# Maxima ahead of scores: the order of two matmul pairs, and of the PSUM banks they take, in a two-layer transformer block

## The chip, the cores and the metric

The kernel runs on one core of a Trainium2 chip. The metric is the device time of one execution in microseconds (us). TensorE (PE) multiplies, VectorE (DVE) and ScalarE (ACT) read PSUM, GpSimd (POOL) works in SBUF and starts indirect DMAs, SyncE (SP) starts the other DMAs.

## The reference

Four sequences of 512 tokens of width 128 go through two layers. Each is `x = x + attention(layernorm(x)) + ffn(layernorm(x))`:

```
scores = einsum('bhqe,bhke->bhqk', q, k) * scale        # 16 heads of width 8
attn   = softmax(scores, axis=-1)                       # layer 1: with a block mask of 64x64 blocks
out    = einsum('bhqk,bhke->bhqe', attn, v) -> projection
layer 0 ffn: silu(x @ wg.T) * (x @ wu.T) @ wd.T         # 384 hidden, weights int / 127
layer 1 ffn: 8 experts, top 2 per token, at most CAP tokens per expert, 256 hidden each
```

Everything stays in f32 accuracy: q and k are held as sums of three bf16 parts.

## The kernel before, in words

One sequence in one layer is a **unit** u (0 to 3 are layer 0, 4 to 7 layer 1). A unit has 16 **slots**: four groups of heads (s) by four blocks of 128 keys (k). A slot has two **halves** (jj = 0, 1), and each half makes

- a **score** pair (`score_mms`, L733): two matmuls, keys on the partitions, 512 queries, from 59 rows of KO and QO. Three of the rows of QO carry minus the row maximum, so that ACT's exponential (`exponential`, L946, 128x1024 in one instruction) gives the softmax numerators in `PT`;
- a **maxima** pair (`max_mms`, L718): two matmuls, queries on the partitions, 512 keys, whose row maxima DVE takes (`read_max`, L1098, a reduce of 128x1024). These maxima belong to work 24 pairs (12 slots) ahead: from slot 4 of unit u on they are those of unit u + 1. In unit 7 only slots 0 to 3 have maxima.

Between the two halves PE multiplies the numerators of the slot before by the values (`value_mms`, L749, 8 matmuls); it waits for both exponentials of that slot. After the second half stands the slot's side work: transposes, q and k of a later unit (L681), output products, values of the next unit (L687 or L692), and in slots 9 to 11 of layer 0 the gate and up products (L771, L772; DVE's L1119 and L1134 use them). From slot 4 of unit 6 on each slot also holds two jobs of the experts (L778, L788, L789, L796; ACT's L969, L962, L978).

PSUM has eight banks. Bank 6 holds the values product, bank 7 the side work. The other six are three **pairs of banks**, handed out in turn: `taken` lists all jobs (scores, maxima, gates, expert jobs) in PE's order, the i-th takes pair i % 3, and `take_pair` makes PE wait until the job three places before it in the list has been read: a score by ACT's exponential (`exp_done`), a maxima pair by DVE's reduce (`max_read`), a gate job by DVE's last product (`h_ready`).

DVE and ACT have their own fixed orders, which the change leaves alone. In each slot DVE reads the first maxima, then does the side work that the slot has (softmax normalization in slots 2 and 11, residual in 7, layernorm statistics in 8, values in 9, router logits in 13), reads the second maxima, then does the gate products. ACT does the first exponential, side copies, and the second exponential. SP's queue starts the DMAs in one order: operand rows, rows of the maxima (L431), mask rows (L425), and in unit 0 the clearing of the expert buffers (L338, L341).

Of the kernel before, what the change touches and what calls it, by code (L numbers as in the profile page):

```python
# [17 lines left out]
def build(nc, x, wq, wk, wv, bq, bk, bv, wo, bo, wg_T, wu_T, wd_T, src_blocks, tgt_blocks, router_T, eg_T, eu_T,  # L18
# [33 lines left out]
    with ExitStack() as ctx:  # L52
# [191 lines left out]
        SLOTS_U = 16  # L244
# [6 lines left out]
        def layer(u):  # L251
            return u // B
# [12 lines left out]
        def rows_of(t, half, j, rows, blocks):  # L265

            return t[64 * half:64 * half + rows, j, blocks[0] * P:blocks[1] * P]

        def reads_of(u):

            return 16 * sum(4 if layer(v) == 0 else 32 for v in range(u % 3, u + 1, 3))

        def pairs_at(u, slot):

            q = LEAD + PAIRS_U * u + 2 * slot
            return [v for v in (q, q + 1) if v < N_PAIRS]

        def gate_at(u, slot):

            return HB * u + slot - 9 if u < B and 9 <= slot < 9 + HB else None  # L280
# [12 lines left out]
        def expert_work_at(u, slot):  # L293

            a = 2 * (SLOTS_U * (u - (U - 2)) + slot - EXPERTS_FROM)
            return expert_work[a:a + 2] if a >= 0 else []
# [6 lines left out]
        taken = [("max", q) for q in range(LEAD)]  # L303
        for u in range(U):
            for slot in range(SLOTS_U):
                for jj in range(2):
                    taken.append(("score", 2 * (SLOTS_U * u + slot) + jj))
                    if len(pairs_at(u, slot)) > jj:
                        taken.append(("max", pairs_at(u, slot)[jj]))
                if gate_at(u, slot) is not None:  # L310
                    taken.append(("gate0", gate_at(u, slot)))
                taken += expert_work_at(u, slot)
# [5 lines left out]
        def take_pair(pe, kind, n):  # L318

            i = turn[kind, n]  # L320
            if i >= 3:
                before, m = taken[i - 3]
                left = {"score": exp_done, "max": max_read, "gate0": h_ready[0], "gate1": h_ready[1],
                        "places": places_ready, "expert": y_copied}[before]
                pe.wait_ge(left, m + 1)
            return i % 3
# [376 lines left out]
        def max_mms(pe, q):  # L703
            u, m = q // PAIRS_U, q % PAIRS_U
            s, qt, jj = m // 8, m % 8 // 2, m % 2
            if m == 0:
                if u == 0:
                    pe.wait_ge(first_rows, 16 * 4)
                else:
                    pe.wait_ge(qk_rows[u % 3], reads_of(u))  # L710
                if B <= u < B + 3:
                    pe.wait_ge(mask_rows, 32 * (u - B + 1))
            if q == PAIRS_U // 2:
                pe.wait_ge(qk_rows[0], reads_of(0))
            pair = take_pair(pe, "max", q)
            rows = PROD_ROWS if layer(u) == 0 else M_ROW
            for half in range(2):
                mm = pe.matmul(ps[:, 2 * pair + half, :], rows_of(QO[u % 3], half, 2 * s + jj, rows, (qt, qt + 1)),  # L718
                               rows_of(KO[u % 3], half, 2 * s + jj, rows, (0, NT)), start=True, stop=True)
            mm.then_inc(max_ps, 1)  # L720
# [8 lines left out]
        def score_mms(pe, u, slot, jj):  # L729
            s, k = slot // 4, slot % 4  # L730
            pair = take_pair(pe, "score", 2 * (SLOTS_U * u + slot) + jj)
            for half in range(2):
                mm = pe.matmul(ps[:, 2 * pair + half, :],  # L733
                               rows_of(KO[u % 3], half, 2 * s + jj, ROWS, (k, k + 1)),
                               rows_of(QO[u % 3], half, 2 * s + jj, ROWS, (0, NT)), start=True, stop=True)
            mm.then_inc(st_ps, 1)

        def value_mms(pe, t):
            u, slot = t // SLOTS_U, t % SLOTS_U
            s, k = slot // 4, slot % 4  # L740
            pe.wait_ge(exp_done, 2 * t + 2)
            if slot == 0:
                pe.wait_ge(v_read, u + 1)
                if u >= 1:
                    pe.wait_ge(o_copied, 2 * u)
            if slot == 8:
                pe.wait_ge(o_copied, 2 * u + 1)
            for g in range(4):
                last = pe.matmul(ps[32 * g:32 * g + 32, PV_BANK, :], Vp[u % 2][:, k, head(s, g), :],  # L749
                                 PT[:, (2 * t + g % 2) % 4, g // 2, :],  # L750
                                 start=(s % 2 == 0 and k == 0), stop=(s % 2 == 1 and k == NT - 1))
            last.then_inc(pv_done, 1)
# [13 lines left out]
        def gate_up_0(pe, g):  # L766
            u, i = g // HB, g % HB
            pe.wait_ge(ready, 1)
            pair = take_pair(pe, "gate0", g)
            cols = slice(i * P, (i + 1) * P)  # L770
            pe.matmul(ps[:, 2 * pair, :], wg[:, cols], xnT[u % 4][:], start=True, stop=True).then_inc(gate_ps[0], 1)  # L771
            pe.matmul(ps[:, 2 * pair + 1, :], wu[:, cols], xnT[u % 4][:], start=True, stop=True).then_inc(up_ps[0], 1)  # L772

        def places_mms(pe, e):
            pe.wait_ge(places_in[e % 2], 16 * (e // 2 + 1))
            pair = take_pair(pe, "places", e)
            for j in range(JE):
                last = pe.transpose(across(pair, j * P, (j + 1) * P), places[e % 2][:, j, :], ident[:])  # L778
            last.then_inc(places_ps, 1)

        def gate_up_1(pe, g):

            e, i, c = g // 4, g % 4 // 2, g % 2
            pe.wait_ge(loaded, N_LOAD)
            pe.wait_ge(places_ready, e + 1)
            pair = take_pair(pe, "gate1", g)
            cols, x_T = slice(i * P, (i + 1) * P), places_T[e % 2][:, c * HALF:(c + 1) * HALF]
            pe.matmul(ps[:, 2 * pair, 0:HALF], eg[:, e, cols], x_T, start=True, stop=True).then_inc(gate_ps[1], 1)  # L788
            pe.matmul(ps[:, 2 * pair + 1, 0:HALF], eu[:, e, cols], x_T, start=True, stop=True).then_inc(up_ps[1], 1)  # L789
# [10 lines left out]
        def out_mms(pe, u, tiles):  # L800
            L = layer(u)
            if tiles[0] == 0:
                pe.wait_ge(onT_ready, u + 1)
                if L == 0:
                    pe.wait_ge(h_ready[0], HB * (u + 1))
            for t in tiles:
                tok = slice(t * P, (t + 1) * P)
                last = pe.matmul(ps[:, SIDE, tok], o_T[:, tok], w_proj[L][:], start=True, stop=(L == 1))
                if L == 0:
                    for i in range(HB):  # L810
                        last = pe.matmul(ps[:, SIDE, tok], h0_T[:, i, tok], wd[:, i, :], start=False,  # L811
                                         stop=(i == HB - 1))
            if tiles[-1] == NT - 1:
                last.then_inc(y_ps, 1)
# [70 lines left out]
        def tensor_unit(pe, u):  # L885
            pe.wait_ge(m_rows[0], 16 * M_DMAS * (u + 1))
            for slot in range(SLOTS_U):
                if slot == 8:
                    pe.wait_ge(m_rows[1], 16 * M_DMAS * (u + 1))
                maxima = pairs_at(u, slot)  # L890
                score_mms(pe, u, slot, 0)
                if maxima:
                    max_mms(pe, maxima[0])
                if u > 0 or slot > 0:
                    value_mms(pe, SLOTS_U * u + slot - 1)
                if slot == 6 and u >= 1:
                    pe.wait_ge(mT_ready, 2 * u + 2)
                    out_mms(pe, u - 1, (0, 1))
                score_mms(pe, u, slot, 1)
                if maxima:  # L900
                    max_mms(pe, maxima[1])
                if gate_at(u, slot) is not None:
                    gate_up_0(pe, gate_at(u, slot))
                for kind, n in expert_work_at(u, slot):
                    if kind == "places":
                        places_mms(pe, n)
                    elif kind == "gate1":
                        gate_up_1(pe, n)
                    else:
                        expert_out(pe, n)  # L910
                side_mms(pe, u, slot)
# [507 lines left out]
        def _(pe):  # L1419
# [27 lines left out]
            for u in range(U):  # L1447
                tensor_unit(pe, u)
# [52 lines left out]
```

## Time and profile before

| | us |
|---|---|
| median of 3 runs | 556.64 |
| lowest and highest | 556.34, 560.81 |
| the profiled execution: its time | 560.18 |
| the profiled execution: its span | 558.2 |

In the span PE is busy 82%, DVE 72%, ACT 59%, POOL 47%. The first 69 us load, lay out q and k of the first units and find the first maxima; the 128 slots run from there to about 520 us; the end gathers the experts' results. Matmuls are pipelined: a PE row's length holds its latency, so the distance from one start to the next tells what it costs.

### The profile page before, as it was taken

All of it is one profiled execution on the core that took longest, in us unless ns stands there. A gap on an engine that the chain in (4) does not pass through costs nothing.

```text
span 558.2 us, 9308 instructions
## 1 busy us (share of the span) xinstructions
PE 456.9 (82%) x3394; PEld 170.5 (31%) x3394; DVE 401.1 (72%) x535; ACT 328.4 (59%) x422; POOL 260.8 (47%) x502
## 2 busy tenths in 40 slices
PE   3165298989798899889988988898799999999952
PEld 2011022223332243224322422232135444555511
DVE  3589479987588879886898698779877877723304
ACT  2100267677357766776676567767776676667560
POOL 6525039104843537377728775786210333063240
PEclk9755599999799999999999999999999999999995
DMA  1698964589970045153615363445650111010018
GB/s 52 177 203 135 123 225 143 86 87 105 243 140 4 1 122 56 18 65 130 69 12 68 129 69 32 57 143 70 77 99 26 49 47 50 1 44 26 20 43 216
DMA packets 156511, 48.28 MB, mean 86 GB/s; under 512 B 115170, under 2 KB 153586, under 8 KB 155634
## 3 DMA queue, kind: packets, MB, share of 16 engines
q1 hardware_dynamic: 154162, 42.93, 43.1%
q0 software_dynamic: 2304, 4.76, 2.6%
q8 instruction: 27, 0.44, 0.3%
q14 instruction: 18, 0.15, 0.1%
HBM read 22.81 MB, written 23.14 MB: 82 GB/s over the span
## 4 chain that ended last, share of the span: by engine, by line
PE 48%; DVE 12%; SPq 11%; issue 10%; ACT 9%; DMA 7%; POOL 2%; POOLq 0%; ACTq 0%; DVEq 0%
PE ps L749 12%; PE ps L733 8%; PE ps L718 6%; ACT PT L946 6%; DVE mx L1098 5%; PE ps L788 3%; PE ps L796 3%; SPq L338 2%; PE ps L771 2%; DMA QO<-mT 2%; PE ps L789 2%; PE ps L681 2%; SPq L420 2%; PE ps L811 1%; PE ps L772 1%
## 5 line engine op out<-in xcount | busy, mean ns | idle before, releaser
L1098 DVE TENSOR_REDUCE mx<-ps 128x2 f32<-128x1024 f32 x256 | 309.5, 1222 | 86.4 <-PE ps L718 78.0
L946 ACT ACTIVATE PT<-ps 128x1024 f32<-128x1024 f32 x256 | 258.3, 1025 | 135.6 <-PE ps L733 126.6
L749 PE MATMUL ps<-PT,Vp 128*32 128x512 f32 x1024 | 138.1, 611 | 5.4 <-ACT PT L946 4.4
L718 PE MATMUL ps<-KO,QO 48*128 48x512 bf16 (+1 forms) x512 | 104.3, 407 | 45.4 <-ACT PT L946 22.0
L733 PE MATMUL ps<-QO,KO 59*128 59x512 bf16 x512 | 100.5, 391 | 13.7 <-DMA QO<-mT 13.7
L507 POOL DMA_INDIRECT y_tokens<-y_sb,meta x40 | 38.5, 963 | 71.6 <-ACT y_sb L978 48.4
L733 PEld LDWEIGHTS ps<-QO,KO 59*128 59x128 bf16 x512 | 24.6, 93 | 151.9 <-issue 96.3
L532 POOL CAST mp<-mx 128x32 bf16<-128x32 f32 x16 | 3.4, 214 | 100.1 <-DVE mx L1098 95.9
L718 PEld LDWEIGHTS ps<-KO,QO 48*128 48x128 bf16 (+1 forms) x512 | 25.5, 96 | 77.5 <-ACT PT L946 38.3
L1119 DVE SCALAR_TENSOR_TENSOR th<-th,ps 128x320 f32<-128x320 f32 (+1 forms) x44 | 23.8, 541 | 35.2 <-ACT th L962 29.4
L496 POOL DMA_INDIRECT x_places<-xe,place_i x32 | 31.9, 995 | 21.9 <-ACT PT L946 15.8
L749 PEld LDWEIGHTS ps<-PT,Vp 128*32 128x32 f32 x1024 | 20.4, 108 | 46.3 <-issue 40.4
L962 ACT ACTIVATE th<-ps 128x320 f32<-128x320 f32 (+1 forms) x44 | 21.1, 486 | 12.0 <-PE ps L788 5.5
L788 PE MATMUL ps<-places_T,eg 128*128 128x320 f32 x64 | 24.4, 463 | 2.2 <-ACT y_sb L978 0.7
L1134 DVE SCALAR_TENSOR_TENSOR h_all<-th,ps 128x320 f32<-128x320 f32 (+1 forms) x44 | 23.8, 541 | 1.5
L479 POOL TENSOR_SCALAR xe<-xs,mv,rstd 128x128 f32<-128x128 f32 x28 | 22.2, 804 | 0.8 <-POOL rstd L470 0.2
L789 PE MATMUL ps<-places_T,eu 128*128 128x320 f32 x64 | 22.4, 432 | 0.0
L978 ACT ACTIVATE y_sb<-ps,meta 128x128 f32<-128x128 f32 x40 | 11.2, 371 | 18.7 <-PE ps L796 18.7
L796 PE MATMUL ps<-ed,h_all 128*128 128x128 f32 x160 | 19.4, 276 | 1.2 <-DVE h_all L1134 1.2
L796 PEld LDWEIGHTS ps<-ed,h_all 128*128 128x128 f32 x160 | 18.9, 192 | 3.0 <-DVE h_all L1134 1.7
L939 ACT COPY mT<-ps 24x512 bf16<-24x512 bf16 x16 | 9.0, 561 | 16.2 <-PE ps L725 16.2
L1104 DVE RECIPROCAL rden<-ps 128x32 f32<-128x32 f32 x16 | 5.6, 348 | 16.8 <-PE ps L757 16.8
(167 smaller groups left out, 477.8 us busy)
## 6 DMA issues: line engine op xcount, KB each, us to landing
z<-part SPq DMA_DIRECT2D x16, 384.0 KB
z<-part SPq DMA_DIRECT2D x16, 256.0 KB
QO<-z SPq DMA_DIRECT2D x64, 48.0 KB
KO<-z SPq DMA_DIRECT2D x64, 48.0 KB
x_places<-zero_f SPq DMA_DIRECT2D x8, 320.0 KB, 10.0
places<-x_places SPq DMA_DIRECT2D x8, 320.0 KB, 3.6
QO<-z SPq DMA_DIRECT2D x6, 384.0 KB
KO<-z SPq DMA_DIRECT2D x6, 384.0 KB
```

Of the source, the lines that this page charges most:

```text
L496: pool.indirect_dma_start(out=x_places[:], out_offset=bass.IndirectOffsetOnAxis(ap=place_i[:, b, t, k:k + 1], axis=0), in_=xe[p % 2][:, t, ...
L507: pool.indirect_dma_start(out=y_tokens[:], out_offset=bass.IndirectOffsetOnAxis(ap=meta[:].bitcast(I32)[:, e, j, 0:1], axis=0), in_=y_sb[e ...
L718: mm = pe.matmul(ps[:, 2 * pair + half, :], rows_of(QO[u % 3], half, 2 * s + jj, rows, (qt, qt + 1)), rows_of(KO[u % 3], half, 2 * s + jj, ...
L733: mm = pe.matmul(ps[:, 2 * pair + half, :], rows_of(KO[u % 3], half, 2 * s + jj, ROWS, (k, k + 1)), rows_of(QO[u % 3], half, 2 * s + jj, R ...
L749: last = pe.matmul(ps[32 * g:32 * g + 32, PV_BANK, :], Vp[u % 2][:, k, head(s, g), :], PT[:, (2 * t + g % 2) % 4, g // 2, :], start=(s % 2 ...
L788: pe.matmul(ps[:, 2 * pair, 0:HALF], eg[:, e, cols], x_T, start=True, stop=True).then_inc(gate_ps[1], 1)
L789: pe.matmul(ps[:, 2 * pair + 1, 0:HALF], eu[:, e, cols], x_T, start=True, stop=True).then_inc(up_ps[1], 1)
L796: last = pe.matmul(across(pair, j * P, (j + 1) * P), h1_T[:, e % 2, i, j * P:(j + 1) * P], ed[:, e, i, :], start=(i == 0), stop=(i == EB - 1))
L946: act.activation(PT[:, e % 4], ps[:, 2 * pair:2 * pair + 2, :], ACT.Exp).then_inc(exp_done, 1)
L1098: dve.tensor_reduce(mx[:, a, qt, col:col + 5:4], ps[:, 2 * pair:2 * pair + 2, :], AX_X, ALU.max, negate=True).then_inc(max_read, 1)
L1119: dve.scalar_tensor_tensor(out=t, in0=t, scalar=1.0, in1=ps[:, bank, 0:n], op0=ALU.add, op1=ALU.mult).then_inc(gate_done[L], 1)
L1134: dve.scalar_tensor_tensor(out=dst, in0=t, scalar=0.5, in1=ps[:, bank + 1, 0:n], op0=ALU.mult, op1=ALU.mult).then_inc(h_ready[L], 1)
```

## The change

In each half of a slot the maxima pair is issued ahead of the score pair, and `taken` lists them in that order. The values product stays between the halves, the side work after them. Where a slot has no maxima nothing moves.

```diff
             for slot in range(SLOTS_U):
                 for jj in range(2):
-                    taken.append(("score", 2 * (SLOTS_U * u + slot) + jj))
                     if len(pairs_at(u, slot)) > jj:
                         taken.append(("max", pairs_at(u, slot)[jj]))
+                    taken.append(("score", 2 * (SLOTS_U * u + slot) + jj))
...
                 maxima = pairs_at(u, slot)
-                score_mms(pe, u, slot, 0)
                 if maxima:
                     max_mms(pe, maxima[0])
+                score_mms(pe, u, slot, 0)
                 if u > 0 or slot > 0:
                     value_mms(pe, SLOTS_U * u + slot - 1)
...
-                score_mms(pe, u, slot, 1)
                 if maxima:
                     max_mms(pe, maxima[1])
+                score_mms(pe, u, slot, 1)
```

PE's queue in slots 14 and 15 of unit 1, where there is no side work (L733 scores, L718 maxima, L749 values; in brackets the semaphores that the instruction waits for; "x3" is that many alike). Before:

```order
L733 MATMUL ps<-QO1,KO1 128x512 [waits max_read]
L733 MATMUL ps<-QO1,KO1 128x512
L718 MATMUL ps<-KO2,QO2 128x512 [waits exp_done]
L718 MATMUL ps<-KO2,QO2 128x512
L733 MATMUL ps<-QO1,KO1 128x512 [waits max_read]
L733 MATMUL ps<-QO1,KO1 128x512
L718 MATMUL ps<-KO2,QO2 128x512 [waits exp_done]
L718 MATMUL ps<-KO2,QO2 128x512
L749 MATMUL ps<-PT,Vp1 32x512 [waits exp_done]
L749 MATMUL ps<-PT,Vp1 32x512 x3
```

With the change, the same place:

```order
L718 MATMUL ps<-KO2,QO2 128x512 [waits exp_done]
L718 MATMUL ps<-KO2,QO2 128x512
L733 MATMUL ps<-QO1,KO1 128x512 [waits max_read]
L733 MATMUL ps<-QO1,KO1 128x512
L718 MATMUL ps<-KO2,QO2 128x512 [waits exp_done]
L718 MATMUL ps<-KO2,QO2 128x512
L733 MATMUL ps<-QO1,KO1 128x512 [waits max_read]
L733 MATMUL ps<-QO1,KO1 128x512
L749 MATMUL ps<-PT,Vp1 32x512 [waits exp_done]
L749 MATMUL ps<-PT,Vp1 32x512 x3
```

The kinds of semaphore stay with the kinds of matmul, but not how far back they reach. Before, a score waits for the reduce of the maxima two halves back, and a maxima pair for the exponential of the half before. Now a maxima pair waits for the exponential two halves back, and a score for the reduce of the half before.

PE's queue from the second half of slot 9 of unit 1 to the gate products of slot 10 (L771 and L772 are the gate and up products, `h_ready0` is set by the last DVE product of a gate job). Before:

```order
L771 MATMUL ps<-xnT1,wg 128x512 [waits max_read,ready]
L772 MATMUL ps<-xnT1,wu 128x512
L733 MATMUL ps<-QO1,KO1 128x512 [waits exp_done]
L733 MATMUL ps<-QO1,KO1 128x512
L718 MATMUL ps<-KO2,QO2 128x512 [waits max_read]
L718 MATMUL ps<-KO2,QO2 128x512
L749 MATMUL ps<-PT,Vp1 32x512 [waits exp_done]
L749 MATMUL ps<-PT,Vp1 32x512 x3
L733 MATMUL ps<-QO1,KO1 128x512 [waits h_ready0]
L733 MATMUL ps<-QO1,KO1 128x512
L718 MATMUL ps<-KO2,QO2 128x512 [waits exp_done]
L718 MATMUL ps<-KO2,QO2 128x512
```

With the change:

```order
L771 MATMUL ps<-xnT1,wg 128x512 [waits exp_done,ready]
L772 MATMUL ps<-xnT1,wu 128x512
L718 MATMUL ps<-KO2,QO2 128x512 [waits max_read]
L718 MATMUL ps<-KO2,QO2 128x512
L733 MATMUL ps<-QO1,KO1 128x512 [waits exp_done]
L733 MATMUL ps<-QO1,KO1 128x512
L749 MATMUL ps<-PT,Vp1 32x512 [waits exp_done]
L749 MATMUL ps<-PT,Vp1 32x512 x3
L718 MATMUL ps<-KO2,QO2 128x512 [waits h_ready0]
L718 MATMUL ps<-KO2,QO2 128x512
L733 MATMUL ps<-QO1,KO1 128x512 [waits max_read]
L733 MATMUL ps<-QO1,KO1 128x512
```

The gate products wait for the slot's first exponential now and no longer for the reduce of its first maxima; the score ahead of the next gate products waits for that reduce instead.

## Rows read from the trace of the kernel before

**Rows 1.** The page, span in 40 slices of 14 us: TensorE's granted clock in tenths.
```profile
PEclk9755599999799999999999999999999999999995
```

**Rows 2.** The page, costliest groups: xcount | busy us, mean ns | idle before, releaser.
```profile
L1098 DVE TENSOR_REDUCE mx<-ps 128x2 f32<-128x1024 f32 x256 | 309.5, 1222 | 86.4 <-PE ps L718 78.0
L946 ACT ACTIVATE PT<-ps 128x1024 f32<-128x1024 f32 x256 | 258.3, 1025 | 135.6 <-PE ps L733 126.6
```

**Rows 3.** Waits of the whole span: us in total, times, longest.
```profile
PE ps L718 <- ACT PT L946: 22.0, 40, 0.8
PE ps L718 <- DVE mx L1098: 9.5, 16, 1.7
```

**Rows 4.** Timeline 288 to 292 us (unit 3, slots 14 and 15; unit 4, slot 0): start, length, engine, line.
```profile
288.05 0.39 PE L733 MATMUL ps<-QO,KO 59*128 59x512 bf16 x2
288.28 0.38 PE L718 MATMUL ps<-KO,QO 56*128 56x512 bf16 x2
288.48 1.02 ACT L946 ACTIVATE PT<-ps 128x1024 f32<-128x1024 f32 x1
288.50 0.38 PE L733 MATMUL ps<-QO,KO 59*128 59x512 bf16 x2
288.70 2.52 DVE L1098 TENSOR_REDUCE mx<-ps 128x2 f32<-128x1024 f32 x2 [0.31 <-PE ps L718]
...
289.56 0.39 PE L718 MATMUL ps<-KO,QO 56*128 56x512 bf16 x2 [0.68 <-ACT PT L946]
289.88 1.06 PE L749 MATMUL ps<-PT,Vp 128*32 128x512 f32 x8
290.88 0.39 PE L733 MATMUL ps<-QO,KO 59*128 59x512 bf16 x2
```

**Rows 5.** Timeline, DVE's side work in slots 7 and 8 of unit 2, PE's in 8.
```profile
205.56 0.68 DVE L1142 TENSOR_TENSOR xs<-ps,xs 128x512 f32<-128x512 f32 x1
...
208.42 0.86 DVE L1053 BATCH_NORM_STATS2 stats<-xs 128x6 f32<-128x128 f32 x4
208.67 1.16 PE L687 MATMUL ps<-w_v,xnT 128*128 128x128 f32 x8
209.32 0.38 DVE L1059 BATCH_NORM_AGGREGATE mv<-stats 128x2 f32<-128x6 f32 x4
```

**Rows 6.** Timeline, gate products of slots 9 and 10 of unit 2.
```profile
212.08 1.10 PE L771 MATMUL ps<-xnT,wg 128*128 128x512 f32 x2 [0.18 <-DVE mx L1098]
...
215.18 2.35 DVE L1098 TENSOR_REDUCE mx<-ps 128x2 f32<-128x1024 f32 x2
...
216.54 1.10 PE L771 MATMUL ps<-xnT,wg 128*128 128x512 f32 x2 [0.43 <-DVE mx L1098]
```

**Rows 7.** Timeline, DVE and PE in slots 9 and 10 of unit 4.
```profile
326.22 1.13 DVE L1081 TENSOR_TENSOR Vp<-ps,b_v 128x64 f32<-128x64 f32 x8
...
327.27 4.70 DVE L1098 TENSOR_REDUCE mx<-ps 128x2 f32<-128x1024 f32 x4
327.80 1.07 PE L749 MATMUL ps<-PT,Vp 128*32 128x512 f32 x8
```

**Rows 8.** The chain that ended last, slot 2 of unit 4: start, us, what.
```profile
298.73 1.23 DVE mx L1098
...
300.80 1.12 PE ps L681 x2
```

**Rows 9.** Timeline, slots 11 and 12 of unit 6, after an expert's results.
```profile
447.65 1.40 ACT L978 ACTIVATE y_sb<-ps,meta 128x128 f32<-128x128 f32 x5 [2.33 <-PE ps L796]
...
450.02 0.39 PE L718 MATMUL ps<-KO,QO 56*128 56x512 bf16 x2 [0.52 <-ACT PT L946]
```

**Rows 10.** The chain that ended last, unit 1: SP's queue ahead of slot 8.
```profile
145.97 2.81 DMA QO<-mT
```

**Rows 11.** Timeline: the values product behind that wait, and a mask wait in unit 3.
```profile
149.79 1.93 PE L749 MATMUL ps<-PT,Vp 128*32 128x512 f32 x8
...
248.21 0.39 PE L718 MATMUL ps<-KO,QO 56*128 56x512 bf16 x2 [0.60 <-DMA QO<-mask_q]
```

## The prediction, made before the changed kernel ran

> **What bounds the kernel now.** I read the page's busy shares first: PE is at 82%, but no engine is full. The granted clock is at 2.4 GHz in all slices from the 13th to the last but one [rows 1], so matmuls have a fixed price there. Then I read the costliest groups: DVE's reduce of the maxima is the longest reader of PSUM, 1222 ns against 1025 ns for the exponential [rows 2]. The waits say who holds PE today: a maxima pair waits for the exponential 40 times, 22.0 us in all, and for a reduce 16 times, 9.5 us [rows 3]. Last I read one stretch of slots without side work as a timeline [rows 4], for the period of a slot and what closes it.
>
> In that stretch a slot lasts 2.83 us (score at 288.05, again at 290.88). Its links: the second score starts at 288.05; its exponential starts 0.43 later and lasts 1.02 to 1.04; the next maxima pair starts 0.05 after that end, at 289.56; the values product 0.32 later, at 289.88; the next second score 1.00 later. 0.43 + 1.04 + 0.05 + 0.32 + 1.00 = 2.84. PE's own work in such a slot is two times (0.22 + 0.22), plus 0.1 for the step to the values, plus 1.00, so 1.98 us; the rest is that wait. **The loop score, exponential, maxima, values closes a plain slot.** A reduce takes 1.26 (2.52 for two) and starts 0.43 after its matmuls; it is read without hurry, because nothing waits for it before two halves have passed.
>
> **The change, part by part.** No instruction is added or removed. Writing M for maxima, S for scores, V for values, a slot becomes M S V M S, then side work.
>
> *The exponential's tight link goes.* M now waits for an exponential two halves back, which is long done. V still waits for the second one, but with S later by one pair. That loop is now V 1.00, M 0.22, S 0.43, exponential 1.04, 0.05: 2.74 us, 0.09 less than today.
>
> *The reduce's tight link comes.* The first S of a slot waits for the reduce of the second M of the slot before. That loop: V 1.00, second M and 0.43 to its reduce, the reduce 1.26, 0.05, S, 0.32 to V: 3.06, say 3.05 us. It is the longer one, so a plain slot costs **+0.22**. By itself this does not depend on PE's work. With side work X on PE after the second half the slot is the larger of 3.05 and 1.98 + X, against the larger of 2.83 and 1.98 + X before; from X = 1.07 on nothing changes.
>
> Now the kinds of slot, each walked with these links. DVE is idle 0.55 us in a new plain slot (3.05 less two reduces), so its side work D between the two reduces delays the second one only by what is over that.
> - Plain or nearly so: 30 slots (some others drop out, below): 30 x 0.22 = 6.6. Slot 3 has a copy on ACT and takes 2.92 today: 5 x 0.13 = 0.65.
> - Slots 1 and 2 together. M of slot 2 is now issued one S earlier, and the normalization on DVE, for which q's product waits (reduce at 298.73, product at 300.80 [rows 8]), is reached sooner: with V of slot 1 at 0, its second M is at 1.00, the reduce of that 1.43 to 2.68, the reduce of slot 2's first M 2.68 to 3.92, normalization (0.83) to 4.75, the product from 4.80 for 1.12, M 5.92, S 6.14, V of slot 3 at 6.45; today the product starts 5.02 after that V (at 295.78 in unit 4), 0.2 later, of which 0.15 is left. Three times: -0.45. Unit 6 has no such product and pays 0.5.
> - Slot 7: the residual, 0.68 on DVE [rows 5], behind output products after which DVE has no work in store. M at 0, its reduce 0.43 to 1.67, residual to 2.35, second reduce to 3.60, S 3.65, V 3.97 less the first V at 0.53: 3.44 against 2.83, **+0.61**, in 4 units: 2.44.
> - Slot 8: statistics, 0.86 + 0.38 and a gap, 1.28 [rows 5]: second reduce ends 3.38 after V, next V at 3.75 against 3.16: +0.6 in units 0 and 2: 1.2. In units 3 and 4 the values of the next unit take longer on PE than this: 0.
> - Slots 9 to 11 of layer 0. The gate products no longer wait for the reduce of the first M (0.18 and 0.43 [rows 6]), but S ahead of them does. The circle gate products, tanh, two DVE products, reduce of M, gate products takes 4.46 today (212.08 to 216.54); now S and 0.38 stand between the reduce and the gate products, less the 0.05 to 0.1 there was: 4.76. So -0.19 twice for slot 9, then +0.31, +0.33 and, since the reduce behind the last gate job is late too, +0.25 for slot 12, four times each: 3.2.
> - Slot 9 of units 4 and 5: values with bias, 1.13 on DVE [rows 7]. Today the second reduce ends at about 328.5 and V at 327.80 does not wait for it; then it must: 328.5 + 0.05 + 0.31 = 328.86, +1.06, twice: 2.1. Slot 11 there (normalization): +0.05 and +0.5.
> - Slot 13 with router logits, 0.4 on DVE: +0.32 four times: 1.3.
> - The 16 slots with maxima and expert jobs: the second job waits for the reduce of the second M, not for the exponential, and S for the reduce late behind gate products: +0.3 in eleven. After an expert's result copies (1.40 on ACT [rows 9]) M waits 0.52 for an exponential today and will not: -0.3 in five. +1.8.
> - What drops out: delays ahead of a wait that SP's queue sets. In unit 1 the rows of the maxima land at 148.78 (145.97 + 2.81 [rows 10]), whatever slots 0 to 7 take; in unit 3 slot 4 waits 0.60 for mask rows [rows 11]. I count nothing for these slots and the last one or two before. Unit 7 from slot 4 on has no maxima: 0.
>
> Sum: 6.6 + 0.65 - 0.45 + 0.5 + 2.44 + 1.2 + 3.2 + 2.1 + 0.55 + 1.3 + 1.8 = **19.9 us**, against the profiled execution's own 560.18: 580.1. The median of the runs, 556.64, lies 3.5 below that execution; the difference added to it gives 576.5. I say **577**.
>
> The bounds of the one link that no row shows, S behind the reduce: its end to the start of S could be 0.05 (as behind the exponential) or nothing beyond the row's own 1.22; between 2.98 and 3.06 for the slot. With 0.15 instead of 0.22 a slot and half of the DVE terms the sum is 11; with all drop-outs paid (14 slots, 3 us) and 0.6 in each expert slot it is 30. The second end is the less likely, the first also; I stay at 20, nearest to the rows at 288 us.
>
> **The rivals.**
> *Faster.* The reduce might not close the loop. If it ended within 1.36 us of its M's start instead of 0.43 + 1.26 = 1.69, the exponential's loop of 2.74 would decide and the removed waits would be a gain: 0.09 in some 60 slots and the gate products' waits, -6 to -8, 549 us. For it speaks that the exponential is today's most frequent wait; against it that every reduce row has over 1.2 us, as do the row means. Chance 0.05.
> *No change to speak of.* The delays could be swallowed by DMA waits everywhere, as in units 1 and 3: then the sum would be under 5.6. Only two such waits are in the trace, and slots 9 to 15 of all units lie behind them: 0.05.
> *Much slower.* PE gets new pauses of 0.2 to 0.5 us in every slot. Today it pauses up to 0.68 there [rows 4] with the clock at 2.4 GHz [rows 1]; after a DMA wait the values product took 1.93 instead of 1.06 us [rows 11], 1.2 GHz. If the pauses brought that level in 60 slots, at 0.9 us each, it would be +54: 630 us. The Trainium skill (TensorE: Matmul & The Clock Gate, A second HAM failure mode: psum-queue depth-cycling) describes a kernel that cycles through PSUM banks and whose small pauses made the clock swing between its two levels; by that, this case would come. The pauses of today's trace did not do it. Chance 0.03; and 0.03 for 590 to 600 by more DVE lateness than I counted.
>
> **Numbers.** My forecast has 0.84: its own range 565 to 589, which the bounds of 11 and 30 fill with 2 us of spread between runs. The range for 8 in 10 is the same, 565 to 589. A change of under 1% can't be told from none here. Faster 0.05, same 0.05, slower 0.90.
>
> **What the profile would show.** Plain slots at 3.05 us from values product to values product, with S starting 0.05 behind a reduce's end; waits "L733 for DVE L1098" well above 60 times, "L718 for ACT L946" nearly gone; slots 7 and 8 of unit 2 at 3.4 and 3.75; gate products 4.76 apart; DVE's reduces in the chain that ended last with a larger part of the time than the exponentials. Slot 8 of unit 1 should still wait for SP. I am wrong if plain slots stay at 2.83 or below, or if the clock row shows fives between 80 and 520 us.

## The result: slower by 3.8%, and the profile after

| | before | changed |
|---|---|---|
| median, us | 556.49 (4 runs) | 579.78 (577.77 to 580.29, 4 runs) |
| ratio, 95% interval | | 1.0377 (1.0337 to 1.0416) |
| profiled execution, time and span | 560.18, 558.2 | 580.29, 578.3 |

The forecast was 577 in 565 to 589, slower. The profiled executions stand 20.1 us apart, for which the sum had 19.9. The medians stand 23.3 us apart: the profiled execution of the kernel before lies 3.7 us above its median, that of the changed kernel 0.5. One execution of the kernel before in a later session took 850.61 us, and no ratio below uses it.

The page of the changed kernel, chain that ended last, by engine and by line:

```profile
PE 41%; DVE 26%; issue 11%; SPq 8%; DMA 6%; ACT 6%; POOL 2%; POOLq 0%; ACTq 0%; DVEq 0%
DVE mx L1098 17%; PE ps L749 11%; PE ps L733 7%; PE ps L718 6%; PE ps L796 3%; PE ps L788 3%; SPq L338 2%; PE ps L681 2%; DVE th L1119 2%; PE ps L771 2%; DMA QO<-mT 2%; ACT th L962 2%; DVE h_all L1134 2%; PE ps L789 1%; PE ps L811 1%
```

The reduce of the maxima (L1098) was 5% of that chain and is 17%; the exponential was 6% and is no longer among the lines listed. The page's groups and the clock, answering to [rows 1, 2]:

```profile
PEclk9665599999799999999999999999999999999985
...
L1098 DVE TENSOR_REDUCE mx<-ps 128x2 f32<-128x1024 f32 x256 | 305.3, 1221 | 98.7 <-PE ps L718 95.7
L946 ACT ACTIVATE PT<-ps 128x1024 f32<-128x1024 f32 x256 | 261.8, 1027 | 159.2 <-PE ps L733 151.3
...
L733 PE MATMUL ps<-QO,KO 59*128 59x512 bf16 x512 | 99.6, 387 | 37.7 <-DVE mx L1098 34.4
```

Nothing takes longer (1221 and 1027 ns, for 1222 and 1025), and the clock row has no five between 80 us and the last slice, as before. What is new is PE's idle time ahead of the scores. The waits of the whole span (us, times, longest), answering to [rows 3]:

```profile
PEld ps L733 <- DVE mx L1098: 63.9, 81, 2.0
...
PE ps L733 <- DVE mx L1098: 34.4, 62, 1.5
...
PEld ps L718 <- ACT PT L946: 12.9, 14, 1.7
```

The 22.0 us in which a maxima pair waited for an exponential are gone from PE's list; 34.4 us in which a score waits for a reduce have come, in 62 waits (the prediction said well above 60). The timeline of the same place as [rows 4], slot 15 of unit 3 and slot 0 of unit 4:

```profile
298.22 1.06 PE L749 MATMUL ps<-PT,Vp 128*32 128x512 f32 x8
...
299.21 0.39 PE L718 MATMUL ps<-KO,QO 56*128 56x512 bf16 x2
299.44 0.38 PE L733 MATMUL ps<-QO,KO 59*128 59x512 bf16 x2
299.64 2.36 DVE L1098 TENSOR_REDUCE mx<-ps 128x2 f32<-128x1024 f32 x2 [0.68 <-PE ps L718]
299.85 0.39 PE L718 MATMUL ps<-KO,QO 56*128 56x512 bf16 x2
...
300.93 0.39 PE L733 MATMUL ps<-QO,KO 59*128 59x512 bf16 x2 [0.69 <-DVE mx L1098]
301.25 1.07 PE L749 MATMUL ps<-PT,Vp 128*32 128x512 f32 x8
```

Values at 298.22, second maxima 0.99 later, their reduce 0.43 after that, 1.23 long, the next slot's first score 0.06 behind its end, values 0.32 later, at 301.25: 3.03 us. Before it was 2.83. The pause ahead of the score is 0.69 us, as long as the 0.68 that a maxima pair waited before [rows 4].

### The profile page after: what moved, and what is told of

The parts are those of the page before. It is cut to its first block, busy times and chain, and to the rows that moved or that the text cites. A ratio compares the mean times of both kernels' runs of the same rounds, so it can differ in the third digit from the quotient of the medians.

```text
span 578.3 us, 9308 instructions
## 1 busy us (share of the span) xinstructions
PE 464.6 (80%) x3394; PEld 175.8 (30%) x3394; DVE 397.3 (69%) x535; ACT 331.7 (57%) x422; POOL 261.0 (45%) x502
## 4 chain that ended last, share of the span: by engine, by line
PE 41%; DVE 26%; issue 11%; SPq 8%; DMA 6%; ACT 6%; POOL 2%; POOLq 0%; ACTq 0%; DVEq 0%
DVE mx L1098 17%; PE ps L749 11%; PE ps L733 7%; PE ps L718 6%; PE ps L796 3%; PE ps L788 3%; SPq L338 2%; PE ps L681 2%; DVE th L1119 2%; PE ps L771 2%; DMA QO<-mT 2%; ACT th L962 2%; DVE h_all L1134 2%; PE ps L789 1%; PE ps L811 1%
## 5 line engine op out<-in xcount | busy, mean ns | idle before, releaser
L1098 DVE TENSOR_REDUCE mx<-ps 128x2 f32<-128x1024 f32 x256 | 305.3, 1221 | 98.7 <-PE ps L718 95.7
L946 ACT ACTIVATE PT<-ps 128x1024 f32<-128x1024 f32 x256 | 261.8, 1027 | 159.2 <-PE ps L733 151.3
L749 PE MATMUL ps<-PT,Vp 128*32 128x512 f32 x1024 | 139.8, 619 | 5.5 <-ACT PT L946 4.4
L718 PE MATMUL ps<-KO,QO 48*128 48x512 bf16 (+1 forms) x512 | 104.7, 409 | 33.5 <-DMA KO<-z 11.6
L733 PE MATMUL ps<-QO,KO 59*128 59x512 bf16 x512 | 99.6, 387 | 37.7 <-DVE mx L1098 34.4
L718 PEld LDWEIGHTS ps<-KO,QO 48*128 48x128 bf16 (+1 forms) x512 | 24.9, 94 | 168.0 <-issue 99.5
L733 PEld LDWEIGHTS ps<-QO,KO 59*128 59x128 bf16 x512 | 24.9, 94 | 81.9 <-DVE mx L1098 63.9
L749 PEld LDWEIGHTS ps<-PT,Vp 128*32 128x32 f32 x1024 | 20.5, 108 | 46.0 <-issue 37.6
```

The lines of the kernel that those rows point to most:

```text
L733: mm = pe.matmul(ps[:, 2 * pair + half, :], rows_of(KO[u % 3], half, 2 * s + jj, ROWS, (k, k + 1)), rows_of(QO[u % 3], half, 2 * s + jj, R ...
L946: act.activation(PT[:, e % 4], ps[:, 2 * pair:2 * pair + 2, :], ACT.Exp).then_inc(exp_done, 1)
L1098: dve.tensor_reduce(mx[:, a, qt, col:col + 5:4], ps[:, 2 * pair:2 * pair + 2, :], AX_X, ALU.max, negate=True).then_inc(max_read, 1)
```

## Experiments

Each ratio is to the kernel before in the same session on the chip, because the kernel before itself ran at medians of 556.5, 550.5, 554.2, 554.5 and 550.0 us in five sessions. Slot times are from one values product's start to the next.

### Order of issue alone, order of the banks alone

The changed kernel with the old list of banks (`issue_only`), and the kernel before with the new list (`banks_only`):

```diff
 # issue_only, against the changed kernel        # banks_only: the reverse edit on the kernel before
+                    taken.append(("score", 2 * (SLOTS_U * u + slot) + jj))
                     if len(pairs_at(u, slot)) > jj:
                         taken.append(("max", pairs_at(u, slot)[jj]))
-                    taken.append(("score", 2 * (SLOTS_U * u + slot) + jj))
```

> PE issues the maxima pair ahead of the score pair in each half, as the changed kernel, but the list that hands out the banks keeps the score first, as before. Distance theory (what costs is how few PE instructions lie between a pair and the next pair that wants its banks): the first maxima pair of a slot now waits for the exponential of the score pair issued right ahead of it. Loop: 0.43 + 1.04 + 0.05 to the maxima, 0.22 to the score, 0.31 to the values, 1.00, 0.22 back to the score = 3.27 us for a plain slot, against 2.83 before and 3.03 changed; the whole kernel 590 to 605 us. Order theory (what costs is that scores and their exponentials come 0.22 later, whatever the banks): plain slot 3.03, 577 to 580 us.

> PE issues score ahead of maxima, as before, but the list hands out banks with the maxima first. Distance theory: the first score pair of a slot waits for the reduce of the maxima pair issued right ahead of it. Loop: 0.43 + 1.26 + 0.05 to the score, 0.22 to the maxima, 0.32 to the values, 1.00, 0.22 back to the maxima = 3.50 us for a plain slot; the whole kernel 605 to 625 us. Order theory: as before, 556 us.

Measured: `issue_only` 606.73 us, ratio 1.102 (1.0983 to 1.1057); `banks_only` 664.13 us, 1.2063 (1.2005 to 1.212). The order theory, which had 577 to 580 and 556, is out. The distance theory has the sign and the rank, but both are slower than I wrote. The timeline of `issue_only`:

```profile
364.67 0.39 PE L718 MATMUL ps<-KO,QO 56*128 56x512 bf16 x2 [0.15 <-ACT PT L946]
364.90 0.38 PE L733 MATMUL ps<-QO,KO 59*128 59x512 bf16 x2
...
366.24 0.58 ACT L926 COPY xnT<-ps 128x512 f32<-128x512 f32 x1
366.40 0.39 PE L718 MATMUL ps<-KO,QO 56*128 56x512 bf16 x2
...
368.12 0.39 PE L718 MATMUL ps<-KO,QO 56*128 56x512 bf16 x2
```

and of `banks_only`:

```profile
393.36 0.39 PE L733 MATMUL ps<-QO,KO 59*128 59x512 bf16 x2 [0.74 <-DVE mx L1098]
...
395.29 0.39 PE L733 MATMUL ps<-QO,KO 59*128 59x512 bf16 x2 [0.33 <-DVE mx L1098]
...
397.23 0.39 PE L733 MATMUL ps<-QO,KO 59*128 59x512 bf16 x2 [0.49 <-DVE mx L1098]
```

I had walked one half of the slot. The wait stands in **both** halves, and the second hides the values product inside itself: in `issue_only` each half is 0.23 from maxima to score and 1.50 from score to the end of its exponential, 1.73 (364.67, 366.40, 368.12), so a slot of 3.46, the measured figure. In `banks_only` it is 0.22 + 1.71 = 1.93 (393.36, 395.29, 397.23), a slot of 3.86; 3.87 was measured. With both halves walked the distance theory gives these to 0.01 us. That walk was made after the runs, with links read from their own rows. The links of the kernel before come close to it: 0.22 + 0.43 + 1.04 + 0.05 = 1.74 a half with the exponential, and 1.93 with a reduce of 1.23.

`banks_only` also shows TensorE falling to its lower level. Windows of 10 us (busy per engine, granted clock, DMA share, GB/s):

```profile
210.00:220.00 10.00, 8.40 (x36) 1.65 (x36) 5.66 (x7) 4.45 (x5) 2.45 (x8) 0.50 0.00 0
...
300.00:310.00 10.00, 8.31 (x72) 4.71 (x68) 4.57 (x5) 4.79 (x7) 5.50 (x6) 1.00 0.31 104
```

In the first, at 1.2 GHz, slots take 4.7 to 5.2 us instead of 3.87; so 664 lies above the 605 to 625 expected partly for that reason. It isn't the only such stretch: between 120 and 490 us thirteen windows of 10 us have a mean granted clock of 0.50 to 0.88. `issue_only` has one fall, to 0.50 to 0.57 from 350 to 365 us. By the Trainium skill (TensorE: Matmul & The Clock Gate, A second HAM failure mode: psum-queue depth-cycling) small pauses between matmul groups that cycle through PSUM banks make the clock swing. The clock of this trace swings too, but that the pauses cause it is not shown here, since slots with the same order of work and the same pauses also ran at 1.00. The changed kernel's trace, with a pause in one half of its slots only, shows no swing in such slots.

### One half alone

```diff
-                    taken.append(("score", 2 * (SLOTS_U * u + slot) + jj))
-                    if len(pairs_at(u, slot)) > jj:
-                        taken.append(("max", pairs_at(u, slot)[jj]))
+                    both = [("score", 2 * (SLOTS_U * u + slot) + jj)]
+                    both += [("max", v) for v in pairs_at(u, slot)[jj:jj + 1]]
+                    taken += both[::-1] if jj == 0 else both      # jj == 1 in second_half
```

(and PE's calls in that half alone exchanged).

> Only the first half of a slot has maxima ahead of scores (issue and banks): M S V S M. Distance theory: the reduce of the second maxima, now issued last, is wanted by a score after the next values product only; what closes the slot is the exponential of the second score, for which the first score of the next slot waits: 0.43 + 1.04 + 0.05 + 0.32 + 1.00 = 2.84 us, as before; the whole 553 to 559 us. Rival (each swapped half costs its share of the 23 us): 568 us.

> Only the second half of a slot is swapped: S M V M S. Distance theory: the first maxima pair of the next slot waits for the reduce of the second maxima, two PE pairs back: 0.43 + 1.26 + 0.05 + 0.32 + 1.00 = 3.06 us (3.03 measured in the changed kernel for the same links); the whole 574 to 581 us, as the full change. Rival (shares): 568 us.

Measured: `first_half` 561.34 us, 1.0199 (1.0179 to 1.0218); `second_half` 577.97 us, 1.0492 (1.0475 to 1.051). Plain slots: 2.83 and 3.03, both as the distance theory had them. (One slot counted as plain, slot 5, takes 3.00 in `first_half`, where a copy on ACT stands ahead of its second exponential.) So the wait that lengthens the plain slot comes from the second half: once its maxima are issued first, a reduce that began 0.43 us later must end before the next slot can fill that bank. The swap of the first half alone is not free, though, against the 553 to 559 expected: slot 6 of unit 2 takes 6.69 instead of 6.09 and the gate slots 10 and 11 take 5.15 and 4.72 instead of 4.89 and 4.46, the same as in the full change. Those come from the first half. In time the two halves cost 10.8 and 27.5 us against the kernel before in their session, the full change 23.3, so their costs don't add: in `second_half` slots 7 and 8 of unit 2 take 3.44 and 4.02, more than the 3.23 and 3.43 of the full change, and slots 1 and 2 together 6.81, for 6.22. By its total alone `first_half` also fits the rival (568, which is 11.5 above); `second_half` and the plain slots don't.

### The reduce made longer

```diff
             dve.wait_ge(max_ps, q + 1)
+            if q % 2 == 1 and q >= LEAD:
+                dve.memset(pad[:], 0.0)      # pad: 128x160 f32
```

> The kernel before, with a dummy DVE memset of 160 columns (some 0.2 us) between the wait for the second maxima pair of a slot and its reduce, 116 times. Reduce theory (before the change this reduce has slack, two reduces and the memset being 2.7 us of a 2.83 us slot): plain slots stay at 2.83 us, the whole is up 0 to 6 us. Rival (DVE's total work sets the time in both kernels): up 116 times its length, some 20 us or more.

> The changed kernel with the same dummy memset. Reduce theory (this reduce closes the slot): each plain slot longer by the memset's whole length, 3.03 to about 3.23 us; the whole 15 to 25 us above the changed kernel, 595 to 605 us. Rival (the new 20 us come from elsewhere, such as the later scores): 0 to 6 us above it.

Measured in one session: `slow_before` 554.67 us, 1.0007 (0.9994 to 1.0019); `slow_after` 586.15 us, 1.0588 (1.0569 to 1.0607). Before the change a memset of 192 ns ahead of 116 reduces costs nothing, and plain slots stay at 2.83. With the change it is paid. Timeline of `slow_after` (memset L1100, reduce L1101, score L734):

```profile
300.24 0.39 PE L719 MATMUL ps<-KO,QO 56*128 56x512 bf16 x2
...
300.73 0.19 DVE L1100 MEMSET pad<- 128x160 f32 x1 [0.75 <-PE ps L719]
...
300.84 2.29 DVE L1101 TENSOR_REDUCE mx<-ps 128x2 f32<-128x1024 f32 x2
...
302.06 0.39 PE L734 MATMUL ps<-QO,KO 59*128 59x512 bf16 x2 [0.93 <-DVE mx L1101]
```

From maxima to score it is 1.82 us, against 1.72 in the changed kernel: of the 0.19 only about 0.1 lengthens the path. The memset starts 0.49 after the maxima and the reduce 0.11 after the memset, so the reduce starts 0.60 after the maxima instead of 0.43, and from its start to the score it is 1.22 instead of 1.29. Plain slots are 3.14 (+0.11). The expectation of 595 to 605 took the whole length; the kind of effect is right, its size was about half: by the ratios `slow_after` lies some 12 us above the changed kernel (the two ran in different sessions), and its slots add up to 10 us more (slots 7 and 8 of unit 1 left out), for 15 to 25 expected. That is more than the 0 to 6 of the rival.

### The change without the expert slots

```diff
+        def swapped(u, slot):
+            return not expert_work_at(u, slot)
...
+                    taken += both[::-1] if swapped(u, slot) else both
```

> The change in all slots but the 16 with maxima and expert jobs, which keep the order of before. The profile puts 4.4 us of the 20 there (I had predicted 1.8): 575 us if it is so, 578 us if it was 1.8.

Measured: 571.08 us, 1.0331 (1.0298 to 1.0365). That is 16.8 us above the kernel before as timed next to it, where the expectation had 18.5 if the profile's 4.4 were right and 21.5 if it was 1.8. The interval overlaps that of the full change, so the times alone don't settle the share. The slots do: the 16 sum to 86.0 us in the changed kernel, 81.7 before and 81.7 here.

### Versions meant to beat both

`values_early` moves the values product ahead of the first maxima; `split_before` and `split_after` issue column groups 0 and 2 of it between the first half's pairs and groups 1 and 3 behind them; `halved_before` and `halved_after` issue queries 0 to 255 where it stands and 256 to 511 after the second half.

```diff
 # values_early
                 score_mms(pe, u, slot, 0)
+                if u > 0 or slot > 0:
+                    value_mms(pe, SLOTS_U * u + slot - 1)
                 if maxima:
                     max_mms(pe, maxima[0])
-                if u > 0 or slot > 0:
-                    value_mms(pe, SLOTS_U * u + slot - 1)
 # split_*: in value_mms(pe, t, part)
-            for g in range(4):
+            for g in (part, part + 2):
 # halved_*: in value_mms(pe, t, part)
+            cols = slice(part * S // 2, (part + 1) * S // 2)
```

> The kernel before with the values product moved ahead of the first maxima pair: S V M S M; banks unchanged. If the exponential's loop closes a plain slot of before, the 0.32 us between maxima and values leaves it and 0.22 comes in: 0.43 + 1.04 + 0.05 + 1.00 + 0.22 = 2.74 us against 2.83; the whole 549 to 553 us. Rival (the wait is absorbed elsewhere): 556 us.

> The kernel before with the values product in two parts: the two matmuls that need the first exponential of the slot before stand between score and maxima of the first half, the two that need the second one behind the maxima: S Va M Vb S M. The exponential's loop loses half the values product: 0.43 + 1.04 + 0.05 + 0.32 + 0.50 = 2.34 us; then DVE's two reduces, 2.36 to 2.52, close a plain slot: about 2.5 us against 2.83, and PE's pause is filled. The whole 538 to 546 us. If PE or ACT binds instead, 550 or more.

> The changed kernel with the same split: M Va S Vb M S. The reduce's loop: 0.43 + 1.26 + 0.05 + 0.32 + 0.50 = 2.56 us (2.53 with the links as measured), 0 to 0.05 above the split of before in plain slots, more where DVE has side work between its reduces. The whole 542 to 554 us: the change costs 3 to 10 us where it cost 20 to 23, if it is the loop and not the order that costs.

> The kernel before with each values product in two parts of 256 queries, all four column groups in each: one part between the halves as before, one behind the second maxima pair. (Two parts by column group cost twice the time of one product.) If a part costs 0.50 us, the exponential's loop is 0.43 + 1.04 + 0.05 + 0.32 + 0.50 = 2.34 us, and DVE's two reduces, 2.46, close a plain slot: about 2.5 against 2.83. Slots filled by PE get some 0.1 to 0.2 longer by one more step between kinds of matmul and eight more weight loads. The whole 2 to 4% below the kernel before. Rival: a part costs far more than half (as the split by column group did), then 5% or more above.

> The changed kernel with the same halved values product. Distance theory: a reduce ends 1.71 us after its maxima pair, then 0.32 and 0.50 to the next but one maxima pair: 2.53 us for a plain slot, only 0 to 0.07 above the same version with the old order, so the change costs 0.5 to 2% here where it cost 3.8%. If the order of the pairs itself costs (later scores), the gap stays 0.2 us a slot and near 4%.

| | us | ratio (95%) | slots without side work |
|---|---|---|---|
| values_early | 604.46 | 1.0899 (1.086 to 1.0937) | 3.03 |
| split_before | 644.08 | 1.1618 (1.1594 to 1.1642) | 3.05, 3.11 (unit 2, slots 14, 15) |
| split_after | 660.28 | 1.1901 (1.1875 to 1.1926) | 3.04, 3.23 |
| halved_before | 561.17 | 1.0193 (1.0172 to 1.0214) | 2.67, 2.40 |
| halved_after | 590.03 | 1.0714 (1.0689 to 1.0739) | 2.61, 2.60 |

None beats the kernel before. Each taught something.

`values_early`: the move put the first maxima behind the values, so their reduce ends late for the next slot's first score, which takes those banks: 0.43 + 1.23 + 0.05 + 0.32 + 1.00 = 3.03, as measured. Its expectation forgot that a pair that is issued later is also read later. The plain slot is that of the changed kernel, yet the whole is 25 us longer. Part of it lies in slots where DVE has other work (in unit 2 slot 2 takes 4.88 us for 3.78, slot 13 takes 3.87 for 2.83), part in a stretch from 360 to 375 us with a granted clock of 0.50 to 0.65; the rest was not walked.

`split_before`, timeline of the two parts:

```profile
301.55 1.05 PE L749 MATMUL ps<-PT,Vp 128*32 128x512 f32 x4
302.54 0.39 PE L718 MATMUL ps<-KO,QO 56*128 56x512 bf16 x2
...
302.86 1.05 PE L749 MATMUL ps<-PT,Vp 128*32 128x512 f32 x4
```

Two column groups take 1.0 us, as four do (298.22 to 299.21 above). The four run side by side, and a split by groups doubles the price; the chain has PE 76%. `split_after` lies 18.4 us above `split_before` in the profiles, where 3 to 10 were expected. But 7.5 of them are in slots 4 to 15 of unit 7, which have no maxima: there `split_after` puts a score between the two parts and `split_before` leaves them side by side. So this pair of runs doesn't isolate the order, and it is no test of the loops: PE fills its slots.

`halved_before`: a part of 256 columns costs 0.57 to 0.58 (306.27 to 306.85 below), and DVE reads without a pause:

```profile
283.12 10.00 DVE L1104 TENSOR_REDUCE mx<-ps 128x2 f32<-128x1024 f32 x8
...
306.27 0.64 PE L750 MATMUL ps<-PT,Vp 128*32 128x256 f32 x8
...
306.85 0.39 PE L733 MATMUL ps<-QO,KO 59*128 59x512 bf16 x2
```

Plain slots fall to 2.4 to 2.9 us, for about 2.5 forecast, but slots that PE fills, and slot 6, get longer (unit 2: slot 4 3.46 for 3.13, slot 6 6.86 for 6.09, slot 12 3.39 for 3.06) and take back more. In `halved_after` the plain slot is 0.43 + 1.23 + 0.05 + 0.32 + 0.57 = 2.60, as measured; the mean of slots 14 and 15 is 0.07 above `halved_before`. The gap of the totals is 1.0714 / 1.0193 = 1.051, not the 0.5 to 2% I expected: unit 2 takes 60.8 us against 56.7, and of these 4.1 us slots 0, 7, 10, 11 and 12 hold 0.56, 0.53, 0.83, 0.53 and 0.53. By the total, then, the expectation failed, and the rival's near 4% was closer. The waits of the two traces say where the time is:

```profile
PE ps L733 <- DVE mx L1104: 1.6, 4, 0.5
...
PE ps L733 <- DVE mx L1104: 29.2, 82, 0.9
```

The first line is `halved_before`, the second `halved_after`. The 27.6 us more that scores wait for a reduce are nearly the whole gap of 29.0 between the profiled executions. So the link is the one of the distance theory, and what failed was the expectation's walk, which took the plain slots alone: with DVE reading almost without a pause, any other work on it (residual in slot 7, gate products in 10 and 11) delays a reduce for which the next score now waits. In slot 10 of unit 2 one score waits 0.75 us and in slot 11 one waits 0.54. No further run tested this.

## Why the prediction was right, term by term

The slots of unit 2, measured from values product to values product in both profiles. Where the prediction has no term of its own, the forecast is what its rule for side work gives:

| slot | before | changed | difference | forecast |
|---|---|---|---|---|
| 0 | 3.07 | 3.29 | +0.22 | +0.22 |
| 1 and 2 | 6.61 | 6.22 | -0.39 | -0.15 |
| 3 | 2.92 | 3.03 | +0.11 | +0.13 |
| 4 | 3.13 | 3.28 | +0.15 | 0 |
| 5 | 2.83 | 3.03 | +0.20 | +0.22 |
| 6 | 6.09 | 6.69 | +0.60 | 0, not named |
| 7 | 2.83 | 3.23 | +0.40 | +0.61 |
| 8 | 3.16 | 3.43 | +0.27 | +0.6 |
| 9 | 4.21 | 3.99 | -0.22 | -0.19 |
| 10, 11 | 4.89, 4.46 | 5.15, 4.72 | +0.26 each | +0.31, +0.33 |
| 12 | 3.06 | 3.35 | +0.29 | +0.25 |
| 13 | 2.83 | 3.03 | +0.20 | +0.32 |
| 14, 15 | 2.83 each | 3.03 each | +0.2 each | +0.22 |

- **The mechanism** held: the exponential's loop gives way to the reduce's. Shown by the plain slot of 3.03, by `second_half` (that half alone gives it), and by `slow_before` and `slow_after` (slack in one, none in the other). All other links of the two loops are alike, so the plain slot costs what the reduce (1.23) is longer than the exponential (1.02 to 1.04).
- **The plain slot** is +0.20 for +0.22: the reduce releases its banks 1.23 us after its start, not 1.26.
- **DVE's side work** was over-priced: slots 7 and 8 came to +0.40 and +0.27, slot 9 of units 4 and 5 to +0.85 for +1.06. I charged the full length of each DVE row one after the other. But an instruction right behind another starts before the other's row ends: in slot 7 the residual starts 1.15 after a reduce of 1.23, and the next reduce 0.59 after the residual of 0.68 (changed kernel):

```profile
207.60 1.23 DVE L1098 TENSOR_REDUCE mx<-ps 128x2 f32<-128x1024 f32 x1 [1.30 <-PE ps L718]
...
208.75 0.68 DVE L1142 TENSOR_TENSOR xs<-ps,xs 128x512 f32<-128x512 f32 x1
...
209.34 2.35 DVE L1098 TENSOR_REDUCE mx<-ps 128x2 f32<-128x1024 f32 x2
```

  The score so comes 3.45 after the first maxima, not 3.65. For the same reason slots 1 and 2 gave back 0.39 and not 0.15: q's product starts 4.63 after the values product, where the walk had 4.80.
- **Slot 6** was under-priced, at nothing; in the five units that have its output products it costs +0.6 to +0.8. ACT copies the maxima behind the first exponential and the output product waits for that copy. Before (first fence) and changed (second):

```profile
197.30 0.39 PE L733 MATMUL ps<-QO,KO 59*128 59x512 bf16 x2
...
198.22 1.06 PE L749 MATMUL ps<-PT,Vp 128*32 128x512 f32 x8
198.65 0.56 ACT L939 COPY mT<-ps 24x512 bf16<-24x512 bf16 x1
199.26 0.49 PE L808 MATMUL ps<-w_proj,o_T 128*128 128x128 f32 x2
```

```profile
200.70 0.39 PE L733 MATMUL ps<-QO,KO 59*128 59x512 bf16 x2 [0.20 <-DVE mx L1098]
201.02 1.06 PE L749 MATMUL ps<-PT,Vp 128*32 128x512 f32 x8
...
202.06 0.56 ACT L939 COPY mT<-ps 24x512 bf16<-24x512 bf16 x1
202.67 0.49 PE L808 MATMUL ps<-w_proj,o_T 128*128 128x128 f32 x2 [0.58 <-ACT mT L939]
```

  The score went 0.92 us ahead of the values product and now goes 0.32 ahead, so exponential, copy and output product come 0.6 later. The prediction did not walk this path. Its rule lets a slot that PE fills cost nothing, which holds for work behind the second half; these products stand between the halves and wait for the copy. `first_half` shows the same 6.69.
- **The expert slots** came to +4.4 us for +1.8 (`no_experts` brings them back to 81.7). In them PE's waits for a reduce grow from 1.2 us (6 waits of 0.2 us) to 4.9 us (12 waits). One of the changed slots, an expert job behind a late reduce:

```profile
440.14 0.78 PE L788 MATMUL ps<-places_T,eg 128*128 128x320 f32 x2 [0.73 <-DVE mx L1098]
```

- **The sum.** The profiles' difference of 20.1 is made of +16.5 in the attention slots (44 slots that took 2.83 make 10.9 of it), +4.4 in the expert slots, +2.1 in slots without maxima, where nothing was moved (two single slots, each about 1 us longer), and -2.8 ahead of the first values product and behind the last (69.1 and 540.5 us before, 67.4 and 561.8 changed; the slots run to there, not to about 520). The forecast's 19.9 had 18.1 and 1.8: too much in DVE's side work, too little in slot 6 and with the experts. That they cancel is luck, and so is the agreement of 20.1 with 19.9: the +2.1 and the -2.8 don't come from any term of the sum (such slots differ by 1 us between other runs too: slot 15 of unit 7 takes 2.51 us before and 3.59 changed, but 3.59 in `slow_before` and 2.51 in `slow_after`), and by the medians the change costs 23.3.
- **Delays swallowed by SP's queue.** In these two profiles slots 7 and 8 of unit 1 take 11.4 and 10.8 us together, with a DMA wait as in [rows 10, 11], so 0.7 us of the delays ahead of them went there. No other kept profile has this wait: in `slow_before` the two slots take 6.1. The clearing DMAs of the expert buffers land in 10.0 us in the former two and in 7.7 to 8.7 in all others. Whether the change costs more where the wait is absent stays open, since the full change was not run in such a session. `no_experts` was, and its 16.8 us with the 4.4 of the expert slots are 21.2, not more than 23.3. The +4.9% of `second_half` doesn't tell, because its slots 7 and 8 are longer than those of the full change.
- **The rivals.** Faster would have needed a reduce under about 0.93 us; it is 1.22. The lower clock did not come here, but did in `banks_only`, `issue_only` and `values_early`.

## What to carry to other kernels

Where jobs take banks in turn, write down for each reader (wait to start, length, release) how many PE instructions stand between a job and the next one that wants its banks, for every position in the period, then compare the loops; the slower reader belongs where that distance is longest, and here this was the order before. Walk all halves and both ends of each move: three expectations above (`issue_only`, `banks_only`, `values_early`) were off for having walked one only, and `halved_after` for having walked the plain slots only. A cheap test of whether a reader has slack is to make it longer by a known amount in both versions.

## What the runs showed of the hardware that I had not expected

- Four f32 matmuls of 32 columns, each on its own 32 output partitions, take 1.0 us for 512 columns; two of the four take 1.0 us too. Halving the columns instead gives 0.57 to 0.58.
- On DVE an instruction right behind another starts before the other's row ends: 0.11 after a memset of 0.19, 0.59 after a residual of 0.68, 1.15 after a reduce of 1.23. The memset lengthened the path by 0.1 only.
- With pauses in both halves of each slot the granted clock fell to 0.50 (210 to 220 us in `banks_only`, 355 to 360 us in `issue_only`) and came back to 1.00 with the same order of work; what decides it stays open.
